# Macaron block with two expert layers on one core: results three tiles behind, sends spread out, and a last stage with its down products three steps behind

## What is computed

```
x = x + 0.5 * ffn(layernorm(x))
x = x + attention(layernorm(x))        # 16 heads of 8, relative positions
x = x + 0.5 * ffn(layernorm(x))

def ffn(x):
    normed = layernorm(x) * gamma + beta
    top_v, top_i = top_k(softmax(normed @ router_w.T), 2)       # of 8 experts
    gates = softmax(top_v)
    comb = sum(one_hot(top_i, 8) * gates[..., None], axis=1)
    for e in range(8):
        out += comb[:, e, None] * swiglu(normed, gate_up_w[e], down_w[e])   # 384 hidden
    return out + swiglu(normed, shared_gate_up_w, shared_down_w)            # 128 hidden
```

## Time and profile before

| | |
|---|---|
| time, median of 3 runs | 2274.42 us (2271.9 to 2279.68) |
| time of the profiled execution | 2267.75 us |
| its span | 2265.8 us |
| mean granted clock of TensorE | 0.959 of full speed |
| PE busy | 2055.6 us, 91% of the span |
| DVE busy | 1849.0 us, 82% |
| ACT busy | 1351.1 us, 60% |
| POOL busy | 1336.5 us, 59% |
| scatters of the first dispatch, L390 | 128, 124.5 us |
| scatters of the first layer's results, L400 | 142, 0.96 us each |
| scatters of the second layer's results, L1421 | 142, 139.4 us |

### The profile page before, as it was taken

One profiled execution on the slowest core, in us unless ns is written; L12 is line 12 of the kernel. 1 busy time (PEld: TensorE's weight loads), 2 busy tenths in 40 slices (PEclk: granted clock), 3 DMA queues, 4 the chain that ended last, 5 costly groups with the idle time before them and its releaser, 6 DMA issues. The chain is left out here.

```text
span 2265.8 us, 64247 instructions
## 1 busy us (share of the span) xinstructions
PE 2055.6 (91%) x22864; PEld 1244.0 (55%) x22865; DVE 1849.0 (82%) x3842; ACT 1351.1 (60%) x3301; POOL 1336.5 (59%) x1961
## 2 busy tenths in 40 slices
PE   7664988996799999999999999999999997889968
PEld 4443988893344444444444444444444447889965
DVE  6543755667699999999999999999999995666648
ACT  4332544556766766666677667667666655445545
POOL 3665155553355557757757667667577583465554
PEclk8666999999999999999999999999999999999989
DMA  5222242217801111210111011012102104232226
GB/s 158 75 67 84 64 151 88 73 50 232 209 13 34 34 26 19 45 34 13 43 34 45 11 38 49 4 39 48 34 12 44 40 24 156 60 89 74 68 63 185
DMA packets 161414, 149.02 MB, mean 66 GB/s; under 512 B 51602, under 2 KB 135698, under 8 KB 160594
## 3 DMA queue, kind: packets, MB, share of 16 engines
q1 hardware_dynamic: 141984, 109.36, 18.6%
q0 software_dynamic: 17280, 35.56, 4.8%
q10 hardware_dynamic: 1874, 0.51, 0.1%
HBM read 86.76 MB, written 62.55 MB: 66 GB/s over the span
## 5 line engine op out<-in xcount | busy, mean ns | idle before, releaser
L1521 PE MATMUL ps_scores<-c_relw,arena_stats 64*64 64x512 f32 x4096 | 956.5, 598 | 0.0
L1972 ACT ACTIVATE arena_probs<-ps_scores,neg_max 128x512 f32<-128x512 f32 x1024 | 697.0, 684 | 393.6 <-DVE neg_max L1857 389.7
L1857 DVE TENSOR_REDUCE neg_max<-ps_scores 128x1 f32<-128x512 f32 x1024 | 650.0, 662 | 26.9 <-PE ps_scores L1521 24.6
L1509 PE MATMUL ps_scores<-arena_rows,arena_stats 64*64 64x512 f32 x2048 | 483.6, 598 | 5.6 <-ACT arena_probs L1972 3.7
L1509 PE MATMUL ps_scores<-c_batch,arena_stats 64*64 64x512 f32 x2048 | 475.3, 596 | 4.7 <-POOL arena_stats L1449 2.6
L1521 PEld LDWEIGHTS ps_scores<-c_relw,arena_stats 64*64 64x64 f32 x4096 | 277.0, 132 | 247.3 <-issue 185.1
L1654 DVE STREAM_TRANSPOSE arena_weights<-arena_probs 128x1024 f32<-128x1024 f32 x256 | 313.5, 1224 | 1.8 <-ACT arena_probs L1972 1.8
L1654 DVE STREAM_TRANSPOSE arena_results<-arena_probs 128x1024 f32<-128x1024 f32 x256 | 313.2, 1224 | 0.0
L1447 POOL TENSOR_TENSOR arena_stats<-arena_rows,c_mask 128x128 f32<-128x128 f32 x256 | 121.9, 476 | 193.2 <-PE ps_scores L1521 191.6
L1447 POOL TENSOR_TENSOR arena_stats<-c_batch,c_mask 128x128 f32<-128x128 f32 x256 | 121.5, 475 | 193.5 <-PE ps_scores L1521 192.3
L1421 POOL DMA_INDIRECT expert_out<-arena_results,f2x_to x142 | 139.4, 982 | 120.8 <-PE ps_scores L1577 73.7
(11 more groups left out here) (323 smaller groups left out, 4225.9 us busy)
## 6 DMA issues: line engine op xcount, KB each, us to landing
qkv_record<-f1c_rec SPq DMA_DIRECT2D x16, 768.0 KB, 3.9
c_batch<-dispatched SPq DMA_DIRECT2D x71, 129.0 KB
arena_rows<-dispatched SPq DMA_DIRECT2D x71, 129.0 KB
c_batch<-qkv_record SPq DMA_DIRECT2D x32, 256.0 KB
arena_rows<-qkv_record SPq DMA_DIRECT2D x32, 256.0 KB
f2c_Y<-expert_out SPq DMA_DIRECT2D x28, 256.0 KB, 3.3
c_Os<-expert_out SPq DMA_DIRECT2D x20, 256.0 KB, 4.1
f1c_Y<-expert_out SPq DMA_DIRECT2D x16, 256.0 KB, 4.3
```

Source lines behind the costliest of these rows:

```text
L1509: m = nc.tensor.matmul(out, SK[n // 2 % NS][p, h, :, :].rearrange("p h a -> p (h a)"), KT[q][p, h, :], start=True, stop=False)
L1521: m = nc.tensor.matmul(out, SR[n // 2 % NS][p, h, :, :].rearrange("p h a -> p (h a)"), R[p, w0:w0 + L], start=False, stop=True)
L1857: reduce_max(nmx[U % NPAIR][:, n % 2:n % 2 + 1], psS[U % NPAIR][n % 2][:], AX, negate=True).then_inc(s_mx, 1)
L1972: nc.scalar.activation(Pr[s][:, n % 2, :], psS[s][n % 2][:], ACT.Exp, bias=nmx[s][:, n % 2:n % 2 + 1], accum_out=rs[:, G % 2, tt:tt + 1]). ...
```

## The change

It has five parts.

1. First dispatch: before, the second batch of pair p waits for a transpose of the next pair as it begins and for its logits in its middle. Now the 16 scatters of a pair are taken in eight twos (`at` = 0 to 7), and except in the last pair at 1 waits for the next pair's transposes, 2 for its logits, 3 for its choice; except in pair 0 and the last, 4 waits for its ranks, 5 and 6 for the first half and all of its row numbers.
2. First layer's results: the lag is 3 for every tile.
3. Second layer's expert tiles: the last pair's 16 scatters go out in two of every three tiles, n = 13 to 35.
4. End of the attention block: POOL and SP no longer wait for the results to be in HBM; SP waits for them in `finish`, and all loads of `finish` are issued there.
5. `finish`: the hidden products have four buffers, down products stand three steps behind gate and up, DVE computes hidden products three steps ahead of the gated sum, and all four normalizes of a step are ACT's. Normalized rows, transposes, silu and hidden products lie in one piece of SBUF.

```diff
...
@@ -380,23 +381,32 @@
                 wait(pool, (s_E, KE * (p + 1)))
                 for s in (2 * p, 2 * p + 1):
                     wait(pool, (s_nb, KB * (s + 1)), (s_sc[s % 4], SC * (s // 4)))
-                    if s % 2 == 1 and p + 1 < PAIRS:
-                        wait(pool, (s_tp, s + 2))
                     for j in range(JT):
+                        at = JT * (s % 2) + j
+                        if p + 1 < PAIRS:
+                            if at == 1:
+                                wait(pool, (s_tp, 2 * p + 3))
+                            elif at == 2:
+                                wait(pool, (s_lg, 2 * p + 4))
+                            elif at == 3:
+                                wait(pool, (s_D, KD * (p + 2)))
+                        if 0 < p and p + 1 < PAIRS:
+                            if at == 4:
+                                wait(pool, (s_rk, p + 2))
+                            elif at in (5, 6):
+                                wait(pool, (s_E, KE * (p + 1) + KE // 2 * (at - 4)))
                         for k in range(TOPK):
                             t = JT * s + j
-                            if k == 0 and s % 2 == 1 and j == JT // 2 and p + 1 < PAIRS:
-                                wait(pool, (s_lg, s + 3))
                             pool.indirect_dma_start(xd, bass.IndirectOffsetOnAxis(idx[:, k, t:t + 1], 0),
                                                     n0[k][s % NR][:, j, :], None).then_inc(s_sc[s % 4], 16)
             for n in range(ET):
-                q, y, lag = n % 4, n % YR, max(3, 15 - n // 4)
+                q, y = n % 4, n % YR
                 wait(pool, (s_to, n + 1), (s_y, n + 1), (s_st[q], 16 * NS * (n // 4)))
                 for g in range(NS):
                     if g == 0:
-                        pool.wait_ge(x_gu, min(ET, n + lag))
+                        pool.wait_ge(x_gu, min(ET, n + 3))
                     else:
-                        pool.wait_ge(s_tx, min(ET, n + lag + 2))
+                        pool.wait_ge(s_tx, min(ET, n + 5))
                     pool.indirect_dma_start(yd, bass.IndirectOffsetOnAxis(to[y][:, g:g + 1], 0), Ys[y][:, g, :],
                                             None).then_inc(s_st[q], 16)
             for q in range(4):
...
@@ -1351,12 +1361,6 @@
                 sp.wait_ge(s_sn[q], SCB * (B // 4))
             for n in range(NA_B, ET):
                 load_rows(Step(n // XR8, n % XR8, XR8))
-            for q in range(4):
-                sp.wait_ge(s_st[q], 16 * NG2 * ((ET - q + 3) // 4))
-            yv = yd[0:TOPK * TOK, :].rearrange("(k n p) d -> p k n d", k=TOPK, p=P)
-            for s in range(2):
-                for k in range(TOPK):
-                    sp.dma_start(R2["Y"][s][k], yv[:, k, tokens(s), :]).then_inc(R2["s_ga"][s], 16)
...
@@ -1415,8 +1419,9 @@
                     if g == 0:
                         pool.wait_ge(x_gu, min(ET, n + 3))
                     else:
-                        if 0 <= n - LATE < TOPK * JP:
-                            send(LASTP, n - LATE)
+                        at = n - LATE
+                        if at >= 0 and at % 3 < 2 and at // 3 * 2 + at % 3 < TOPK * JP:
+                            send(LASTP, at // 3 * 2 + at % 3)
                         pool.wait_ge(s_tx, min(ET, n + 5))
                     pool.indirect_dma_start(yd, bass.IndirectOffsetOnAxis(to[y][:, g:g + 1], 0), Ys[y][:, g, :],
                                             None).then_inc(s_st[q], 16)
@@ -1468,8 +1473,6 @@
             difference(LASTP)
             for n in range(LATE, ET):
                 result(n)
-            for q in range(4):
-                pool.wait_ge(s_st[q], 16 * NG2 * ((ET - q + 3) // 4))
...
@@ -2038,18 +2041,21 @@
     G1, G2 = R["G1"], R["G2"]
     tag = tag + "c"
     with ExitStack() as c:
+        early = sb(c, f"{tag}_early", [P, 11 * L])
+        homes = [early[:, q * L:(q + 1) * L] for q in range(11)]
+        xn = [home.rearrange("p (j d) -> p j d", j=JT) for home in homes[0:3]]
+        nT, sg, h = homes[3:5], homes[5:7], homes[7:11]
+        assert 11 * L * 4 <= 49152
         Y = R["Y"] + [[sb(c, f"{tag}_Y{q}{k}", [P, JT, D]) for k in range(TOPK)] for q in range(2, NB)]
-        xn = [sb(c, f"{tag}_xn{q}", [P, JT, D]) for q in range(3)]
-        nT, sg, h = ([sb(c, f"{tag}_{x}{q}", [P, L]) for q in range(2)] for x in ("nT", "sg", "h"))
...
         block = c.enter_context(nc.Block())
-        JA = JT - 1
+        HB, AHEAD_H, ROWS = 4, 3, TR // P
...
@@ -2063,7 +2069,9 @@
                 for k in reversed(range(TOPK)):
                     sp.dma_start(Y[s][k][:], yv[:, k, tokens(s), :]).then_inc(s_ga[s % 4], 16)
 
-            for s in range(2, 5):
+            for q in range(4):
+                sp.wait_ge(s_rows[q], 16 * ROWS * ((ET - q + 3) // 4))
+            for s in range(5):
                 wait(sp, (s_cb, JT * (s - 3)))
                 load(s)
             for s in range(NB):
@@ -2085,12 +2093,6 @@
 
         @block.vector
         def _(dve):
-            def normalize(s):
-                t = JT * s + JA
-                wait(dve, (s_tp, s - 2))
-                nc.vector.tensor_scalar(xn[s % 3][:, JA, :], XR[:, t, :], rstd[:, t:t + 1], shift[:, t:t + 1], ALU.mult, ALU.add
-                                        ).then_inc(s_nv, 1)
-
             def gated(s):
...
             def hidden(s):
-                wait(dve, (s_sg, s + 1), (s_gu, s + 1), (s_dn, s - 1))
-                nc.vector.tensor_tensor(h[s % 2][:], psU[s % 2][:], sg[s % 2][:], ALU.mult).then_inc(s_h, 1)
+                wait(dve, (s_sg, s + 1), (s_gu, s + 1), (s_dn, s + 1 - HB))
+                nc.vector.tensor_tensor(h[s % HB], psU[s % 2][:], sg[s % 2], ALU.mult).then_inc(s_h, 1)
...
-            for s in range(2):
-                normalize(s)
-            for s in range(NB + 1):
-                if s + 2 < NB:
-                    normalize(s + 2)
-                if s < NB:
-                    hidden(s)
-                    gated(s)
-                if s >= 1:
-                    shared(s - 1)
+            for s in range(AHEAD_H):
+                hidden(s)
+            for s in range(NB):
+                gated(s)
+                if s + AHEAD_H < NB:
+                    hidden(s + AHEAD_H)
+                shared(s)
 
         @block.scalar
         def _(act):
             def normalize(s):
                 wait(act, (s_tp, s - 2))
-                for j in range(JA):
+                for j in range(JT):
...
         @block.tensor
         def _(pe):
             def transposes(s):
-                wait(pe, (s_n, JA * (s + 1)), (s_nv, s + 1), (s_nT, s - 1))
+                wait(pe, (s_n, JT * (s + 1)), (s_nT, s - 1))
                 for j in range(JT):
                     m = nc.tensor.transpose(psT[s % 2][:, j * P:(j + 1) * P], xn[s % 3][:, j, :], ident[:])
                 m.then_inc(s_tp, 1)
 
             transposes(0)
-            for s in range(NB + 1):
+            for s in range(NB + AHEAD_H):
                 if s + 1 < NB:
                     transposes(s + 1)
                 if s < NB:
                     wait(pe, (s_nT, s + 1), (s_sg, s - 1), (s_h, s - 1))
...
-                if s >= 1:
-                    b = s - 1
+                    nc.tensor.matmul(psG[s % 2][:], sgT[:], nT[s % 2], start=True, stop=True)
+                    nc.tensor.matmul(psU[s % 2][:], suT[:], nT[s % 2], start=True, stop=True).then_inc(s_gu, 1)
+                if s >= AHEAD_H:
+                    b = s - AHEAD_H
...
                     m.then_inc(s_dn, 1)
 
 
```

17 lines of the change are left out of this document (8 added, 9 removed).

## The result

Median of four runs 2258.89 us (2255.98 to 2262.4), against 2276.82 us for four runs of before (2271.9 to 2279.68): ratio 0.9924, 95% interval 0.9898 to 0.995. That is 17.9 us faster, where 43 were forecast, and outside the range (2206 to 2255).

| part | forecast | in the two traces |
|---|---|---|
| A, first expert tiles, results three behind | -23 | -23.1 |
| B, first dispatch | -8 | +11.5 to the last scatter, +11.4 to the fifth tile |
| C, second expert stage | -4 | +2.2 (+0.5 against a second trace of before) |
| D, boundary and last stage | -8 | -2.2 |

What follows compares the result with a forecast made beforehand. TensorE was taken to bound a tile at 3.71 us, with long GpSimd scatter runs delaying other engines' starts. -23 - 8 - 4 - 8 = -43 from the profiled 2267.75 gave 2224.8; 6.7 to the median made 2231 us, range 2206 to 2255.

Steps and rivals of the forecast that it cites:

- A: First expert stage: a constant three-tile lag removes runs of four scatters, leaving 3.71 us per tile; -23 us, bounds 0 and -23.
- B: First dispatch: scatters in waiting twos shorten runs and halve pauses, against a longer last run; -8 us, bounds -25 and +7.6.
- C: Second expert stage: free tiles between three-scatter tiles allow catching up; -4 us, a quarter of 16.2; 0 if each costs 1.02.
- D: Block boundary and last stage: earlier start and no TensorE idle time; -8 us, bounds -3 and -11.
- the chain to the next row numbers: First dispatch: GpSimd pauses at each link towards the next pair's row numbers, so 10 to 12 scatters run together, not 16.
- were to be halved (-16 us): First dispatch: held stretch falls from 10 to 5 us, the pause halves with it; 7 x 2.3 = -16 us.
- +7.6 us for the longer last run: First dispatch's end: 20 to 22 scatters instead of 16 before the first expert tile; up to 6 x 1.26 = +7.6 us.
- bound of B, +7.6: First dispatch, worst case: the pauses stay, or waiting costs as much as it gives; +7.6 us.
- the boundary: Attention block's end: without the wait for results' landing, GpSimd starts the last stage sooner; -1.3 us, 0 if landing still matters.
- it waits with the gated sum for a load: Last stage before the change, at 2211.80: VectorE's gated sum takes 4.80 us because of a load, delaying normalize and transposes.
- a late load stalls only the back end: Last stage: with down products three steps back, TensorE's idle time goes; -8.5 us to the last up product, net -6.9.
- third rival: First dispatch loses: waits stop GpSimd where it ran, final run longer; +7.6 there, second-stage sends 0; 2251 us, chance 0.23.

Runs made afterwards that it cites:

- e1: Kernel before with only the first layer's results three tiles behind at every tile; 2254.48 us, 0.9897 of before.
- h2: Kernel before, unchanged, run again in the third set for a second trace; 2268.4 us (one run).
- e3: Kernel before with only the second dispatch's last-pair sends moved to two of every three tiles; 2274.23 us, 0.9985 of before.
- e4: Kernel before with only the changes to the attention block's end and the last stage (`finish`); 2274.32 us, 0.9987 of before.
- h3: Changed kernel with the first dispatch as before, on a chip that holds starts; 2251.53 us, 0.99 of before.
- e2: Kernel before with only the first dispatch in twos that wait for the next pair; 2285.45 us, 1.0039 of before.
- h1: Changed kernel as it is, run again in the third set; 2259.61 us, 0.9935 of before.
- k1: Changed kernel without the scatters' wait for the next pair's choice, other waits kept; 2252.92 us, 0.9903 of before.
- h4: Changed kernel with pair 6's scatters waiting only for pair 7's transposes and logits; 2259.77 us, 0.993 of before.
- g1: Changed kernel, last-stage loads waiting only until GpSimd took the rows of the step four before; second set's chip, 2135.53 us, 1.0014 of before.
- k4: Changed kernel with the dispatch of before and last-stage loads waiting only for GpSimd; 2248.15 us, 0.9875 of before.
- k5: Changed kernel with before's dispatch, but pair 7's scatters in the first expert tiles, and last-stage loads waiting only for GpSimd; 2248.28 us, 0.9877 of before.
- f1: Changed kernel with the first dispatch as before, on the chip where before takes 2131.78 us; 2128.94 us, 0.9986 of before.

## Why the prediction failed

**What bounds the kernel: right for the chips that hold starts.** Two scatters in a tile cost nothing, a third 1.0 us. That this belongs to the chip could not be read from one trace, and the forecast has no case for it.

**A: right, in mechanism and size.** -23 forecast, -23.1 between the traces, -23.2 in e1.

**B: wrong in sign; the step that failed is "the chain to the next row numbers now finds GpSimd pausing for it at each of its links, and 10 to 12 scatters run together".** After the first pair it pauses mainly at one link. The wait for the transposes is met when GpSimd comes to it, that for the logits mostly too, and so, nearly, are those for ranks and row numbers, which follow the choice by 2 to 5 us; only the choice isn't there. The runs stay at 16 to 18 scatters in most pairs, the stop comes ten scatters earlier, and the pauses, which were to be halved (-16 us), grow from 38 to 42 us in sum (h2, e1, e3, e4, h3) to 45 to 47 (after, e2, h1). I had counted the scatters between two waits in the program, and not those between two waits that bind, and I had left out the first pair, which now has three stops. k1 shows that the wait for the choice makes most of the difference. Why a stop there lasts longer than one at the ranks isn't shown. VectorE makes the choice in some twenty short operations, each behind another's semaphore. Its first, at 157.87, comes 5.0 us after TensorE's last logits (152.87), beside the scatters, and some of the others stand idle for 0.5 to 1.2 us, beside them and in the first 2 us of the stop (two of the six rows above); I take it that the stop waits out this chain, while at the ranks more of it has been done beside scatters that still ran. The +7.6 us for the longer last run stood in the working, and the run is indeed 24 scatters long (26 in h1). In the traces some 5 us lie there, between the last scatter and the fifth tile, but no experiment separates them: h4 left the run as long. The bound of B, +7.6, was too narrow by 1 us.

**C: the mechanism of the -4 is absent.** 16 tiles with a third scatter cost 1.0 us each wherever they stand, the case that I had given as the row's own reading and then left by a quarter. e3: -3.4 us, interval -7.3 to +0.2; its trace shows 292.3 us from the first of the 71 tiles to the last, and the second trace of before 292.4.

**D: the boundary was right (-1.3 forecast, -1.6 to -2.0), the last stage wrong.** Two steps failed. The first is the reading "it waits with the gated sum for a load (4.80 us where 1.12 is usual)". All four sums of that group are held, each until an operation of GpSimd has ended; no load ends any of them. The second is "so a late load stalls only the back end". The back end is the end. TensorE's steps did come 3.05 us apart without the stall, as forecast, until it had used its lead of three steps; then it waited for VectorE, whose own pace is 3.35 us a step, 1.2 of it time in which sums are held. I had put the 7 us of TensorE's idle time to VectorE and not asked what VectorE's pace would be if TensorE's were not in its way. The 16 normalizes taken from VectorE don't show in the stage's length: 66.5 us after, 67.0 before, from TensorE's first transposes to the end. e4 puts boundary and last stage together at 3.3 us (interval 0.2 to 5.9), where 8 were forecast.

The same reading is behind the theories on g1 and k4. In the twelve traces with the new last stage and its loads as in the change, the stage less the time in which sums are held is 51.3 to 51.4 us, while the held time goes from 15.1 to 16.2 us and the stage with it from 66.5 to 67.6. In the three traces with looser loads (g1, k4, k5) the rest is 49.8 to 50.2 us, and the held time 14.1, 17.4 and 17.3. So the looser loads take some 1.3 us off and move GpSimd's operations, which then meet fewer sums or more. No run here kept GpSimd's operations away from VectorE's sums, so what that would gain isn't measured.

**From the profiled execution to the median.** The profiled execution of before lay 6.7 us below its median, that of the changed kernel 1.9. I carried the 6.7 over; part of it was the dispatch, whose last scatter came 5 to 9 us sooner than in other traces and whose fifth tile up to 4 us sooner, in the very stage that the change rewrote.

**The cases.** The third rival, "the dispatch loses" (0.23, 2251), is what happened in B and C; with D's miss beside it the time lay 4 us above the range. That rival's reason (each wait makes GpSimd stop where it ran, and the final run is longer) is borne out. I had joined the bounds of B and C in one case and left D out of it.

## What to carry to other kernels

A wait placed in a queue costs nothing only if it is already met when the queue comes to it, and breaks a run only if it is not: before counting on it, find for each link when it is done and when the queue is there. Where one engine is freed of another by a lead of some steps, ask what the other's own pace is; the stage ends with the slower. An instruction several times as long as its neighbours, with no idle time before it, need not be waiting for data: look at what ended just before it did. And take a second trace before building on a stage whose length changes from run to run, if possible from another chip.

## What the runs showed of the hardware

The kernel met two kinds of chips: before takes 2275.8 to 2277.6 us on the three of the first, third, fourth and fifth set, and 2131.8 us on the one of the second. Matmuls take the same 272 ns on both. On the first kind, releases of VectorE, ScalarE and TensorE come late while GpSimd issues indirect DMAs back to back, for up to 26.6 us in the changed kernel's trace, and TensorE itself crawls in such a run (its products at 211.16, 211.87, 214.80 and 216.92 in the changed kernel, 0.12 us apart elsewhere). On the second, 112 scatters follow one another (f1) and no start of ScalarE is over 2.6 us late. There the Trainium skill's sentence in SBUF — State Buffer, "Who interferes with whom", that "PE and ACT never wait on anyone" agrees with the trace; on the first kind it doesn't describe what is seen. What differs between the chips, and whether the port rule has anything to do with it, no run here shows.

On both kinds, in the last stage, VectorE's gated sums (both tensors in SBUF, 0.34 us alone) stand still while GpSimd multiplies or adds 128x512 floats in SBUF. In the 20 traces 16 to 21 of 64 sums take more than 0.4 us, up to 1.43, and each of them ends 0.15 us after an operation of GpSimd. The operations with one input in PSUM keep their 0.67 to 0.69 us. The profile shows the held time as busy time of VectorE.
